# Value sums of a fused attention kernel: all four key tiles in fp16 halves, one more score slot kept in its bank, and TensorE's waits for older data moved ahead

## The reference, cut to what matters

```
c_q, c_kv = x @ Wq_down, x @ Wkv_down
q_c = (c_q @ Wq_up).reshape(b, s, 128, 4)
q_r = (x @ Wq_rope).reshape(b, s, 128, 64)
k_c, v_c = (c_kv @ Wk_up), (c_kv @ Wv_up)      # 128 heads x 4
k_r = x @ Wk_rope                              # 64, shared by the heads
scores = (q_c . k_c + q_r . k_r) / (4 + 64) ** 0.5
attn = softmax(scores over the keys)
out = (attn @ v_c) @ Wo
```

## Time and profile before

| | |
|---|---|
| median of 3 runs | 2174.14 us (2172.99 to 2179.34) |
| the profiled execution's own time | 2174.77 us |
| its span in the profile | 2173.0 us |
| mean granted TensorE clock | 0.993 of full |
| second attention with halves (first to last ost of sum_pair) | 840 to 1752 us |

### The profile page before, as it was taken

One profiled execution on the slowest core, in us unless ns is written; L12 is line 12 of the kernel. 1 busy time (PEld: TensorE's weight loads), 2 busy tenths in 40 slices (PEclk: granted clock), 3 DMA queues, 4 the chain that ended last, 5 costly groups with the idle time before them and its releaser, 6 DMA issues.

```text
span 2173.0 us, 42690 instructions
## 1 busy us (share of the span) xinstructions
PE 2119.2 (98%) x11276; PEld 1650.1 (76%) x11276; DVE 1739.3 (80%) x3095; ACT 1326.3 (61%) x2709; POOL 1349.8 (62%) x1621
## 2 busy tenths in 40 slices
PE   7999999999999999999999999999999999999978
PEld 4788888888886757777777787777877777777756
DVE  6787788778777758888888888888888877888864
ACT  2443443433433568888888888888888865555532
POOL 4766766766763447777777777777777721455334
PEclk9999999999999999999999999999999999999999
DMA  7010010010004153222222222222222223444351
GB/s 249 26 44 30 20 48 29 19 48 29 19 17 124 37 189 108 78 67 78 75 77 76 67 78 74 78 74 69 78 74 78 78 65 105 113 142 117 103 130 39
DMA packets 138991, 165.82 MB, mean 76 GB/s; under 512 B 30261, under 2 KB 72917, under 8 KB 138916
## 3 DMA queue, kind: packets, MB, share of 16 engines
q1 hardware_dynamic: 135076, 152.31, 24.5%
q0 software_dynamic: 3840, 12.59, 2.0%
HBM read 101.52 MB, written 29.10 MB: 60 GB/s over the span
## 4 chain that ended last, share of the span: by engine, by line
PE 87%; DVE 7%; issue 2%; ACT 1%; POOL 1%; SPq 1%; DMA 1%; DVEq 0%; ACTq 0%; POOLq 0%
PE bank L2609 12%; PE bank L2594 11%; PE bank L2616 11%; PE bank L2171 7%; PE bank L2173 7%; PE bank L2172 7%; PE bank L2526 6%; PE bank L2524 5%; PE bank L2525 5%; PE bank L2626 3%; PE bank L2672 3%; PE bank L2634 2%; DVE rope_b L1640 1%; DVE rope_a L1639 1%; DVE rope_b L1641 1%
## 5 line engine op out<-in xcount | busy, mean ns | idle before, releaser
L1945 DVE TENSOR_REDUCE mcol<-bank 128x1 fp32r<-128x512 f32 x1024 | 690.1, 687 | 173.5 <-PE bank L2594 154.0
L2594 PE MATMUL bank<-km,q 128*128 128x512 f32 x1024 | 416.2, 407 | 4.3 <-ACT q L1377 2.6
L2609 PE MATMUL bank<-q,k 128*128 128x512 f32 x1024 | 413.9, 404 | 0.0
L2616 PE MATMUL bank<-q,k 128*128 128x512 f32 x1024 | 403.3, 394 | 0.0
L2594 PEld LDWEIGHTS bank<-km,q 128*128 128x128 f32 x1024 | 317.1, 310 | 63.9 <-DVE mcol L1945 17.5
L1421 ACT ACTIVATE pT<-bank 128x512 f32<-128x512 f32 x416 | 224.3, 602 | 83.0 <-PE bank L2616 81.3
L850 POOL TENSOR_TENSOR wr_lo<-wst,wr_hi 128x512 fp32r<-128x512 f32 x64 | 82.7, 1292 | 306.1 <-DVE wr_hi L1816 306.1
L1421 ACT ACTIVATE x<-bank 128x512 f32<-128x512 f32 x416 | 227.3, 600 | 44.2 <-PE bank L2616 39.4
L2609 PEld LDWEIGHTS bank<-q,k 128*128 128x128 f32 x1024 | 192.2, 188 | 74.0 <-issue 47.3
L2616 PEld LDWEIGHTS bank<-q,k 128*128 128x128 f32 x1024 | 192.9, 188 | 32.2
L2526 PE MATMUL bank<-hT_hi,wr_lo 128*128 128x512 f32 x512 | 205.7, 402 | 0.0
(11 more groups left out here) (371 smaller groups left out, 4947.6 us busy)
## 6 DMA issues: line engine op xcount, KB each, us to landing
q<-q SPq DMA_DIRECT2D x256, 128.0 KB, 2.3
wst<-in_L_attn_Wq_rope SPq DMA_DIRECT2D x64, 256.0 KB, 3.2
o_d<-ost SPq DMA_DIRECT2D x63, 256.0 KB, 3.1
st_q<-in_L_attn_wq SPq DMA_DIRECT2D x8, 1024.0 KB, 7.6
st_wo<-in_L_attn_wo SPq DMA_DIRECT2D x8, 1024.0 KB, 5.4
q<-qc_d SPq DMA_DIRECT2D x256, 32.0 KB
km<-kc_d SPq DMA_DIRECT2D x256, 32.0 KB
k<-kc_d SPq DMA_DIRECT2D x256, 32.0 KB
```

The lines of the kernel that those rows point to most:

```text
L1945: dve.tensor_reduce(mcol[:, k % 2, i % 4, i // 4:i // 4 + 1], bank[4 + i % 2][:], AX.X, ALU.max, negate=True)\
L2594: pe.matmul(bank[4 + i % 2][:], q2[:, k % 4, h, i % 4:S:4], km[:, b, h], start=True, stop=True).then_inc(max_mm, 1)
L2609: pe.matmul(bank[s % 4][:], k1[:, k % 2, t], q1[:, k % 4, h], start=True, stop=False)
L2616: pe.matmul(bank[s % 4][:], k2[:, k % 2, h, t], q2[:, k % 4, h], start=False, stop=True).then_inc(scores1, 1)
```

## The change

All four key tiles of a halved unit go through the fp16 halves. Slots 6 and 7, too, get a high and a low part, which lie in the space that the exponentials of slots 4 and 5 would have had in PT. Slot 6 is treated as 4 and 5 were: its exponential stays in bank 2, ScalarE copies the high part, VectorE subtracts, and the next unit's slot 2 waits for that. Slot 7 goes to PT; ScalarE copies its high part, and GpSimd subtracts for the low part (last_low). GpSimd learns that the copy is done from q2_hi, which ScalarE raises with the next turn's q_high. The copy of the fp32 values and the memset of their ones go away, as does rest_sums. Waits of slot 0 for loads and low parts of the queries move to the turn before (scores_wait), and those of sum_pair for values, exponentials and the copied bank move ahead of slot 3 (sum_pair_wait).

```diff
-HTILES = 3
-IN_PLACE = (4, 5)
+HTILES = 4
+IN_PLACE = (4, 5, 6)
...
-        halved_part = lambda par, s, i: pH[:, par, s, i] if s < 4 else pH_late[:, par, s - 4, i]
+        halved_part = lambda par, s, i: (
+            pH[:, par, s, i] if s < 4 else pH_late[:, par, s - 4, i] if s < 6
+            else PT[par][:, s - 2].bitcast(F16)[:, i * S:(i + 1) * S])
...
-                pool.tensor_copy(vp[:, kp, HTILES:TB, :, OROWS * kp:OROWS * kp + HD1], full[:, HTILES:TB])
...
+            def last_low(u, par):
+
+                pool.wait_ge(q2_hi, u + 4)
+                pool.tensor_tensor(halved_part(par, 7, 1), PT[par][:, 7], halved_part(par, 7, 0), ALU.subtract).then_inc(p_split, 1)
+
             def halve(u, k, pair):
...
                 if par == 0 and not (isinstance(u, int) and u == 0):
                     values(u, k, pair(0))
                     values(u + 1, k + 1, pair(1))
+                if par == 1:
+                    last_low(u - 1, 0)
                 pool.wait_ge(exp1, 8 * u + (9 if par else 11))
                 for i in range(2, 4):
                     e = pool.tensor_tensor(halved_part(par, i, 1), PT[par][:, i], halved_part(par, i, 0), ALU.subtract)
                 e.then_inc(p_split, 1)
+                if par == 1:
+                    last_low(u, 1)
...
-                            wait(act, p_split, 4 * u - 4)
+                            wait(act, p_split, 5 * u - 6)
...
+                    if s == 7 and exists(u, HALVED):
+                        act.wait_ge(exp1, 8 * u + 12)
+                        act.activation(halved_part(k % 2, 7, 0), PT[k % 2][:, 7], ACT.Copy)
...
+                    pe.wait_ge(exp1, 8 * u + s + 1)
+                    if s + 4 in IN_PLACE and exists(u - 1, HALVED):
+                        pe.wait_ge(p_low, 3 * u - 2 + s)
...
+            def scores_wait(u, k, use, part):
+
+                if exists(u, UNITS):
+                    if part == 0:
                         pe.wait_ge(q1_hi[k % 2], 32 * use + 32)
                         pe.wait_ge(q1_split, u + 1)
+                    if part == 1:
                         pe.wait_ge(m_loaded[k % 2], 32 * use + 32)
+                    if part == 2:
                         pe.wait_ge(k2c_loaded[k % 2], 32 * use + 32)
...
+            def sum_pair(u, k, pair):
+
+                if exists(u - 2, UNITS):
+                    pe.wait_ge(p_split, 5 * u)
+                    pe.wait_ge(p_low, 3 * u)
+                    halved_sums(0, True, False)
+                    halved_sums(1, False, True).then_inc(pv1, 2)
...
                 scores(*turn, range(3))
+                if turn[1] % 2 == 0 and not (isinstance(turn[0], int) and turn[0] > HALVED):
+                    sum_pair_wait(*turn)
...
                     scores(*turn, (5,))
+                scores_wait(turn[0] + 1, turn[1] + 1, turn[2](1), 0)
                 queries(*turn, 1)
...
                     scores(*turn, (6,))
+                scores_wait(turn[0] + 1, turn[1] + 1, turn[2](1), 1)
                 queries(*turn, 2)
                 maximum(*turn, 5)
                 scores(*turn, (7,))
                 maximum(*turn, 6)
+                scores_wait(turn[0] + 1, turn[1] + 1, turn[2](1), 2)
                 queries(*turn, 3)
```

More of the change, by code:

```diff
@@ L860, in zero_others @@
                     ones = slice(OROWS * kp + DEN, OROWS * kp + DEN + HD1)
-                    pool.memset(vp[:, kp, HTILES:TB, :, ones], 1.0).then_inc(zeroed, 1)
                     pool.memset(vpb[:, kp, 0:HTILES, :, ones], 1.0).then_inc(zeroed, 1)
@@ L926, in halve @@
                     pool.tensor_copy(halved_part(par, i, 0), PT[par][:, i]).then_inc(p_split, 1)
-                    pool.wait_ge(p_split, 4 * u + i + 1)
+                    pool.wait_ge(p_split, 5 * u - par + i + 1)
                     e = pool.tensor_tensor(halved_part(par, i, 1), PT[par][:, i], halved_part(par, i, 0), ALU.subtract)
@@ L943, in _ @@
             pool.wait_ge(vc_ready, NT)
-            pool.wait_ge(zeroed, 7)
+            pool.wait_ge(zeroed, 5)
             values(0, 0, 0)
@@ L1887, in _ @@
             key_low(1)
-            dve.wait_ge(zeroed, 7)
+            dve.wait_ge(zeroed, 5)
             dve.wait_ge(vc_ready, NT)
@@ L2599, in scores1_rope @@
                     h, kb = SLOTS[s]
-                    if s == 0:
+                    pe.wait_ge(exp1, 8 * u + s + 1)
+                    if s + 4 in IN_PLACE and exists(u - 1, HALVED):
+                        pe.wait_ge(p_low, 3 * u - 2 + s)
+                    t = slice(kb * P, (kb + 1) * P)
+                    pe.matmul(bank[s % 4][:], k1[:, k % 2, t], q1[:, k % 4, h], start=True, stop=False)
+            def scores_wait(u, k, use, part):
+                if exists(u, UNITS):
+                    if part == 0:
                         pe.wait_ge(q1_hi[k % 2], 32 * use + 32)
                         pe.wait_ge(q1_split, u + 1)
+                    if part == 1:
                         pe.wait_ge(m_loaded[k % 2], 32 * use + 32)
+                    if part == 2:
                         pe.wait_ge(k2c_loaded[k % 2], 32 * use + 32)
[L2605 to L2609, removed]
             def scores1_content(u, k, s):
@@ L2619, in sum_rows, with halved_sums @@
                 return bank[7][32 * group:32 * group + 32, :]
-            def halved_sums(k, opens):
+            def halved_sums(k, opens, closes):
                 for kb in range(HTILES):
@@ L2625, in halved_sums, with sum_pair_wait @@
                         for half in range(2):
[L2626 to L2635, removed]
+                            e = pe.matmul(sum_rows(2 * h + half), vpb[:, k % 2, kb, h], halved_part(k % 2, SLOTS.index((h, kb)), half),
+                                          start=(kb == 0 and opens), stop=(kb == HTILES - 1 and closes))
                 return e
-            def sum_pair(u, k, pair):
+            def sum_pair_wait(u, k, pair):
                 if exists(u - 2, UNITS):
@@ L2663, in sum_unit @@
                     opens, closes = apart or k % 2 == 0, apart or k % 2 == 1
[L2664 to L2672, removed]
+                    for s in range(8):
+                        h, kb = SLOTS[s]
+                        e = pe.matmul(sum_rows(2 * h + kb % 2), vp[:, k % 2, kb, h], PT[k % 2][:, s], start=(s < 4 and opens), stop=(s >= 4 and closes))
                     e.then_inc(pv1, 1)
```

## The result

The changed kernel takes 2227.76 us (median of 4 runs, 2227.35 to 2229.39), the kernel before 2174.55 in the same comparison: 1.0246 times as long, 95% interval 1.0233 to 1.0259. That is +53 us; forecast was +46, with 2220 in a range of 2194 to 2238. The direction and the range held, and the ring (a chain of steps from one event back to the same event one or two pairs later) that set the pace was the one forecast. One stretch of it ran over another engine than forecast, and the size was 13% short.

A forecast was written before the change was run, and what follows sets the result against it. TensorE was taken to bound the kernel before; after the change a ring over VectorE and GpSimd, 20.4 us a pair against 19.42. +0.98 over 47 periods is +46 on 2174.8 us: about 2220, range 2194 to 2238.

The forecast's parts named there:

- TensorE's part: The sums on TensorE: 32 fp16 matmuls take 1.75 us instead of 2.17, so -0.42 a pair.
- The further 0.27 from the moved waits: TensorE's bubbles not behind the sums: moving waits saves at best 0.27 us, giving 18.74 a pair, otherwise 19.0.
- ScalarE's ring: Sums, ost, ScalarE's turns to q_high at 18.7, last_low, next sums: 20.0 us a pair.
- the third ring: Over VectorE's low part of slot 6 and TensorE's slot 2 of the even turn; priced at 0 as hidden.
- VectorE's and GpSimd's ring: Sums to VectorE's cast, GpSimd's work, sums after the next: 40.75 us for two periods, 20.4 each, setting the pace.
- VectorE's half: From the sums over VectorE's reductions and cast to GpSimd's start at L850 in the next period: 22.65 us.
- the first maximum of the odd turn: TensorE stops there for q_high some 0.3 us, which goes into slack.
- slot 2 of the even turn: Matmul waits for VectorE's low part of slot 6, about 18.1 against 17.7 wanted; hidden, otherwise 0.4. A stop here disproves the prediction.
- The gap ahead of the sums: Sign in the profile: one to two us ahead of each sum_pair, released by GpSimd's subtraction of slot 7.
- ScalarE's ring alone: Rival: the cast comes earlier and only ScalarE's 20.0 us (19.9 to 20.2) is left, 2202 us; chance 0.28.
- the engines' free time would hold the copies: Rival: copies fit in idle time, TensorE stays the bound, 18.75 to 19.0 a pair, 2143 to 2155 us; chance 0.07.
- More waits than I see: Rival: TensorE's stops at slot 2 or moved waits delay VectorE; 20.7 and more a pair, 2235 to 2250 us; chance 0.12.

The follow-up runs named there:

- waits_only: The kernel before with only TensorE's waits moved and nothing else of the change: 2173.45 us, ratio 1.0002.
- waits_back: The changed kernel with TensorE's waits where they stood before: 2226.54 us, ratio 1.0240 to the kernel before.
- own_sem: The changed kernel with last_low waiting for a semaphore raised by ScalarE's copy of slot 7, not for q_high: 2230.37 us.
- cast_early: The changed kernel with VectorE's cast of the rotary weights moved to the start of the even turn: 2208.07 us, period 20.16.
- no_low6: The changed kernel without VectorE's subtraction for slot 6, whose low half is left out of the sums: 2213.02 us, period 20.22.

## Why the prediction was right, by its steps

**TensorE's part.** -0.42 us for the sums: measured 1.74 instead of 2.17, right. The further 0.27 from the moved waits: wrong, it is 0 (waits_only; in the changed kernel waits_back). It didn't enter the sum, because TensorE isn't the bound any more, but it would have made the floor 19.0 and not 18.74.

**ScalarE's ring.** 18.7 to the end of q_high: 18.70. The ring of 20.0 over last_low couldn't be seen in the changed kernel itself (own_sem: nothing). With the cast out of the way last_low waited for q_high in every pair, and the trace of cast_early puts this ring at 20.0; there it did not set the pace, since the third ring lies at 20.15 to 20.17 and the period is the same with last_low gone. One link is not as forecast: ScalarE waits 0.41 us for slot 5's scores behind the ost copy (1211.97), so the way from the sums to q_high leads over TensorE's matmuls up to slot 5, and the ost copy has that much to spare.

**VectorE's and GpSimd's ring.** The step that carried the number. What held: GpSimd's half 18.14 against 18.1, the cast as its start (cast_early: -20 us), last_low directly behind other work (own_sem: 0). VectorE's half was 22.93 against 22.65. This is the term that was mis-sized. I subtracted the old wait of 0.25 from VectorE's 15.08 us, on the ground that a late VectorE doesn't wait. It does: 0.19 and 0.24 in the odd turn (in every other pair only the 0.24), because TensorE itself is late there. The 0.28 are 0.14 a period, or 6.6 of the 7 us that were missing.

What makes TensorE late is a wait that the prediction named and priced at nothing: the first maximum of the odd turn waits for q_high, "some 0.3 us, which goes into the same slack". It stops TensorE for 0.38 us (0.28 in every other pair). The profile puts this wait down to VectorE, but the reduction that the kernel asks for there, the seventh, was over at 1216.19; q_high ended at 1217.57, and the first maximum's weights were loaded at 1217.81. In every variant this load follows q_high by 0.12 to 0.24 us. From there to the fourth and fifth maxima TensorE doesn't stop, and VectorE waits for both. So up to the odd unit's fifth reduction this half was not VectorE's own work, as the sum had it, but sums, ScalarE's even turn, q_high, TensorE's maxima; no_low6 shows it, where that reduction comes no earlier with less work on VectorE. By VectorE's waits the two ways are only 0.24 to 0.43 us apart, so the number came out near all the same; that nearness is luck. The stop at slot 2 ahead of it (0.51, for VectorE's own slot 6) lies before the wait for q_high and is covered by it.

**The covers and the signs.** "Hidden" was right for slot 2 of the even turn in the changed kernel as far as the period goes, but I put it with 19.6 some 0.8 us below the period, and it was 0.35 below. The same wait in the odd turn I didn't see at all. The gap ahead of the sums has the releaser that was forecast, but in the weight loads it is 0.70 us here and 0.53 in every other pair, and not one to two; a gap of 0.74 stands at slot 2 of the even turn, which the prediction had named as a sign that it is wrong. By its matmuls TensorE was busy 96% of the stretch and not 92%. The clock stayed at 1.00; a row for a stretch below 95% did exist in the kernel before (650 to 700 us: busy 45.69 of 50 us, granted clock 1.00).

**The rivals.** ScalarE's ring alone would have been 2202; cast_early, which opens the cast's ring, ends at 2208, since the third ring lies 0.15 above ScalarE's. That the engines' free time would hold the copies is refuted: in the stretch ScalarE is busy 88%, VectorE 89%, GpSimd 81%, none is full, and the kernel is 2.5% slower. "More waits than I see" was there, as above, and small. The Trainium skill ("Perfetto Trace Analysis", section "Identifying the Most-Contended Engine") judges TensorE by its weight loads and by its share of peak arithmetic; by the weight loads it has 73% here against VectorE's 89%. That ranks VectorE first, but taking VectorE's new step away (no_low6) won 15 us, and moving a cast of 0.43 us, with no load changed, 20 us. Here the order decided and not the load.

**What stays open.** What holds the last variants at 19.87 to 19.94: the two rings named above are read from traces, and no run opened either. And whether an order exists in which the fp16 halves win: they would need less than 19.42 with the eight more steps a pair (four on ScalarE, two each on VectorE and GpSimd) spread over five rings that lie within 0.7 us of each other.

## What to carry to other kernels

Free time on an engine says nothing about where it lies: follow the ring from an event back to the same event one or two periods later, through every in-order queue, and add up each part; a change pays only if it makes the longest ring shorter. Before counting an engine's wait inside the ring as gone, ask what releases it: where that comes from the same ring, the ring runs over the other engine. When a fix opens one ring, look for the next before counting the whole gain: here four lay within 0.6 us, and the cast moved (20 us), slot 6 left out (15) and the sums split (15) gave 34 us together and not 50. A wait that borrows a later event as its signal (last_low on q_high) costs nothing as long as the engine behind it is late anyway; test it before replacing it.

## What the runs showed of the hardware that was not expected

Waits moved ahead on TensorE's queue, in the kernel before and in the changed one, brought nothing: 2173.45 against 2173.94 us, and 2226.54 against 2227.76 with them moved. The gap at the head of the sums is 0.25 us in the weight loads with five waits in front of it (the kernel before) and with two (waits_only).
